# Weights ahead of biases on SyncE, and two of VectorE's products taken apart, in a routed feed-forward kernel

## The reference

```python
t = t + ffn(layernorm(t), Wg, W1, b1, W2, b2)

def ffn(x, Wg, W1, b1, W2, b2):          # 2048 tokens, D=256, E=8 experts, F=1024, TOP_K=2
    S = sigmoid(xt @ Wg)
    G, I = top_k(S, 2)                   # two experts a token, with their gates
    h = gelu(einsum('nd,edf->enf', xt, W1) + b1[:, None, :])
    y = einsum('enf,efd->end', h, W2) + b2[:, None, :]
    combine = zeros((N, E)).at[arange(N)[:, None], I].add(G)
    return einsum('ne,end->nd', combine, y)
```

## Time and profile before

| what | value |
|---|---|
| median of three executions | 346.78 us (346.38 to 348.04) |
| the profiled execution's own time | 349.64 us |
| its span, first to last instruction | 347.8 us |
| PE busy | 301.3 us, 87% of the span |
| DVE busy | 251.8 us, 72% |
| ACT busy | 182.2 us, 52% |
| POOL busy | 155.1 us, 45% |
| bytes moved by DMA | 39.41 MB, 113 GB/s over the span |

### The profile page before, as it was taken

One profiled execution on the slowest core, in us unless ns is written; L12 is line 12 of the kernel. 1 busy time (PEld: TensorE's weight loads), 2 busy tenths in 40 slices (PEclk: granted clock), 3 DMA queues, 4 the chain that ended last, 5 costly groups with the idle time before them and its releaser, 6 DMA issues.

```text
span 347.8 us, 8621 instructions
## 1 busy us (share of the span) xinstructions
PE 301.3 (87%) x3022; PEld 225.6 (65%) x3022; DVE 251.8 (72%) x597; ACT 182.2 (52%) x506; POOL 155.1 (45%) x161
## 2 busy tenths in 40 slices
PE   0989989999920687999999989999999999999970
PEld 0767833557710366788888868888888888877740
DVE  3786789578899869988887798797855655655530
ACT  3344649444653427558576567667544353554410
POOL 7012770337531360454456354644554635444341
PEclk9989999999975699999999999999999999999996
DMA  7400000002286854367888678789454334233310
GB/s 235 145 1 2 1 0 1 2 0 82 69 288 205 160 164 173 97 148 227 190 206 212 158 168 225 214 183 237 90 90 82 66 73 80 49 69 62 57 17 2
DMA packets 36185, 39.41 MB, mean 113 GB/s; under 512 B 8400, under 2 KB 32816, under 8 KB 36144
## 3 DMA queue, kind: packets, MB, share of 16 engines
q1 hardware_dynamic: 29168, 29.56, 29.5%
q0 software_dynamic: 6976, 9.31, 15.9%
HBM read 29.74 MB, written 9.11 MB: 112 GB/s over the span
## 4 chain that ended last, share of the span: by engine, by line
PE 62%; DVE 16%; DMA 11%; issue 4%; ACT 2%; another core or an unknown queue 1%; SPq 1%; POOL 1%; POOLq 0%; ACTq 0%
PE ps L886 14%; PE ps L871 7%; PE ps L875 7%; PE ps L873 7%; PE ps L887 7%; DMA out<-fb,idx 6%; PE ps L731 5%; PE ps L712 3%; DMA wt<-w 2%; DMA xt<-x_tok 2%; PE ps L740 2%; PE ps L744 2%; PE ps L747 2%; PE ps L825 2%; PE ps L779 1%
## 5 line engine op out<-in xcount | busy, mean ns | idle before, releaser
L659 ACT ACTIVATE fb<-ps,b1t 128x128 f32<-128x128 f32 (+7 forms) x312 | 82.1, 381 | 71.6 <-issue 51.4
L871 PE MATMUL ps<-fb,wt 128*128 128x128 f16 (+7 forms) x624 | 114.4, 214 | 5.3 <-DVE fb L1296 5.3
L886 PE MATMUL ps<-wt,fb 128*128 x312 | 117.0, 379 | 0.0
L875 PE MATMUL ps<-fb,wt 128*128 128x128 f16 (+7 forms) x624 | 114.4, 214 | 0.3 <-issue 0.3
L873 PE MATMUL ps<-fb,wt 128*128 128x128 f16 (+7 forms) x624 | 114.3, 214 | 0.0
L523 POOL DMA_INDIRECT out<-fb,idx x39 | 65.3, 1674 | 101.7 <-DMA out<-fb,idx 69.8
L887 PE MATMUL ps<-wt,fb 128*128 x312 | 85.0, 272 | 0.0
L871 PEld LDWEIGHTS ps<-fb,wt 128*128 x624 | 60.9, 98 | 36.0 <-issue 6.2
L873 PEld LDWEIGHTS ps<-fb,wt 128*128 x624 | 60.4, 98 | 3.3
L875 PEld LDWEIGHTS ps<-fb,wt 128*128 x624 | 60.4, 98 | 0.5 <-issue 0.5
L513 POOL DMA_INDIRECT fb<-xn_rows,idx x39 | 43.6, 1117 | 25.0 <-DVE idx L1274 12.8
(11 more groups left out here) (204 smaller groups left out, 388.1 us busy)
## 6 DMA issues: line engine op xcount, KB each, us to landing
wt<-w SPq DMA_DIRECT2D x32, 512.0 KB
b2t<-b SPq DMA_DIRECT2D x39, 128.0 KB
xt<-x_tok SPq DMA_DIRECT2D x4, 512.0 KB, 7.8
out<-xt SPq DMA_DIRECT2D x8, 256.0 KB, 2.1
xn_rows<-wt SPq DMA_DIRECT2D x8, 256.0 KB, 3.3
b1t<-params SPq DMA_DIRECT2D x39, 4.0 KB
fb<-xn_rows,idx POOLq DMA_INDIRECT x39
out<-fb,idx POOLq DMA_INDIRECT x39, 4.0
```

Source lines behind the costliest of these rows:

```text
L659: a = nc.scalar.activation(hid[:, s, f * P:f * P + ROWS[n]], h_ps(s)[:, f * P:f * P + ROWS[n]], ACT.Gelu_apprx_tanh, bias=b1t[:, n % NBIAS ...
L871: pe.matmul(dst, hi, xT[:, s, c * P:c * P + rows], start=(c == 0 and f % 4 == 0), stop=False, skip_group_check=True)
L875: m = pe.matmul(dst, lo, xT[:, s, c * P:c * P + rows], start=False, stop=(c == DC - 1), skip_group_check=True)
L886: pe.matmul(y_ps(s), hhi[:, s, f * P:(f + 1) * P], w, start=(f == 0), stop=False)
```

## The change

Four edits. SP's opening order becomes pieces 0 and 1, the last rows, the biases of tile 0, pieces 2 and 3, the biases of tiles 1 to 3. In SP's loop the pieces of a tile stand ahead of biases, and the biases are those of tile n + 2 in place of n + 3. `quarters_at(1)` is empty, and piece 4 goes to tile 2's turn beside piece 5, on all three engines that read the function. And `gate_pay` makes one product a call, with `rows_T(3)` between the two calls in VectorE's turn 1; in turn 2 it no longer stands.

```diff
-            upto = lambda n: min(QUARTERS_FIRST + 4 * n // 3, NQ)
+            upto = lambda n: min(QUARTERS_FIRST + 4 * n // 3, NQ) if n != 1 else QUARTERS_FIRST
...
-            for h in range(NSTG):
+            for h in range(DC):
                 load(h)
             rows_out(B - 1)
-            for i in range(NBIAS):
+            biases(0)
+            for h in range(DC, NSTG):
+                load(h)
+            for i in range(1, NBIAS):
                 biases(i)
...
             for n in range(1, TILES):
-                if n + NBIAS - 1 < TILES:
-                    biases(n + NBIAS - 1)
                 for h in quarters_at(n):
                     if h + NSTG < NQ:
                         load(h + NSTG)
+                if NBIAS <= n + 2 < TILES:
+                    biases(n + 2)
...
-            def gate_pay():
+            def gate_pay(n):
-                for n in (2, 3):
-                    ins = v.tensor_tensor(out=pay[:, :, n, :], in0=pay[:, :, 0, :],
-                                          in1=over_tiles(flat(place16[:, n]), 2 * NBLK), op=ALU.mult)
-                ins.then_inc(hot_done, 1)
+                return v.tensor_tensor(out=pay[:, :, n, :], in0=pay[:, :, 0, :],
+                                       in1=over_tiles(flat(place16[:, n]), 2 * NBLK), op=ALU.mult)
...
                 if n == 1:
-                    gate_pay()
-                if 2 <= n < TILES - 1:
+                    gate_pay(2)
+                    rows_T(3)
+                    gate_pay(3).then_inc(hot_done, 1)
+                if 3 <= n < TILES - 1:
                     rows_T(n + 1)
```

## The result

| what | before | after |
|---|---|---|
| median of 20 executions each | 348.93 us (346.38 to 350.87) | 345.76 us (345.06 to 348.82) |
| ratio | 1 | **0.9924** [0.9903, 0.9946] |
| the profiled execution's own time | 349.64 us | 345.52 us |
| its span | 347.8 us | 343.7 us |

The change makes the kernel 0.76% faster, about 2.65 us (1.9 to 3.4 by the interval). This ratio and those of the experiments are the ones on record with their intervals; they are not the quotients of the medians beside them (here 345.76 / 348.93 = 0.9909, or 3.17 us).

The account below looks back on a forecast made before the run. PE sets the pace from about 124 us, with VectorE the bound at the start. Forecast: 346.78 - 0.84 (start) - 0.40 (late weights) = 345.5 us; 8-in-10 range 343.9 to 346.9.

Parts of the forecast that it names:

- The start, 0.84 us: Steps 2 to 4, bound by VectorE: the new order lets step 4 start 0.84 us earlier, bounds 0.3 to 1.15.
- The loop: SP's loop: pieces asked for earlier remove the 1.50 us gap ahead of step 14 in the profiled execution.
- I take 0.4 of late weights in the median: Loop's share of the median: 0.4 us of the 1.50, from three runs' spread of 1.66 us; bounds 0 to 1.5.
- rival B: Every execution has a gap like step 14's, at places with two pieces in one tile; median 344.4 us; chance 27%.
- 3.8 a piece: Tile 12's two weight pieces: 7.6 us from issue to ACT's start on the first, read as 3.8 us each.
- 18 of the 19 waits: ACT's other waits for late weight pieces were hidden behind PE's own step and give nothing.
- The opening order, 0: Start of the kernel: pieces 2 and 3 behind rows and biases cost nothing and gain nothing, taken as 0.
- The biases, late but in time: SP's queue: each bias up to 7.6 us later behind two pieces, still in time with 2 us of cover.
- below 4: Sign of being right: ACT's 15.4 us of waiting for weights fall below 4 us.
- C: Rival: the first gelu waited for its bias, so the earlier bias gives 343.8 us; sign, step 2's gap gone; chance 8%.
- D: Rival: adds land late among weights in flight and delay `scaled`; slower, 349.2 us; chance 7%.
- E: Rival: nothing measurable, the 0.84 us is lost again and late weights are rare; 346.4 to 346.8 us; chance 13%.

Follow-up runs that it names:

- e4: Kernel before with only `rows_T(3)` between the two products of `gate_pay`, piece 4 still in turn 1: 347.71 us against 348.22, 0.9991.
- e5: Changed kernel with `gate_pay` in one piece and `rows_T(3)` back in turn 2, turn 1 still empty: 346.11 us against 348.31 of the kernel before, 0.9957.
- e3: Kernel before with only the empty `quarters_at(1)` and the split `gate_pay`, old loop and old opening: 352.46 us against 348.22, 1.0095.
- e7: Changed kernel, but from tile 5 SP's loop also waits for `scaled(n - 1)` before asking for pieces: 368.34 us against 348.31 of the kernel before, 1.0583.
- e11: The kernel before, unchanged, profiled once more: one execution, 349.98 us.
- e8: Changed kernel with 10 filler products in place of 16 ahead of step 0: 347.20 us against 348.31 of the kernel before, 0.9959.
- e2: Kernel before with only SP's loop changed, pieces ahead of biases and biases of tile n + 2: 346.52 us against 348.22, 0.9937.
- e6: Changed kernel with the old opening order: 347.24 us against 348.31 of the kernel before, 0.9953.
- e1: Kernel before with only the opening order changed: 348.25 us against 348.22, 0.9990.
- e9: Changed kernel, from tile 5 issuing biases of tile n + 2, then waiting for `scaled(n - 1)`, then pieces: 346.67 us against 348.69 of the kernel before, 0.9948.
- e10: Changed kernel with the old loop from tile 5, biases of tile n + 3 and then pieces: 347.75 us against 348.69 of the kernel before, 0.9969.

## Why the prediction was right, and where it was not

**The start, 0.84 us: right in mechanism and size.** A is 28.46 to 28.58 (mean 28.50) in the five profiles with a split in turn 1, and 27.54 to 27.86 (mean 27.67) in the seven without: 0.83 us. The reason holds too: 13.08 us between `rows_T(2)` and the end of `rows_T(4)` on both sides, 12.87 of them VectorE's work. Its signs came as told: the gap ahead of step 3 shrank from 1.29 to 0.26 (0.15 forecast); step 4 comes 142.69 - 137.02 = 5.67 us after step 3, 0.17 more than the 5.50 of the next step; and counted from `rows_T(2)` it is 14.20 - 13.34 = 0.86 us earlier. Not seen was what e4 and e5 show: the empty turn 1 earns all of it, and the two products taken apart, which the title names, earn nothing. Nor did the costing say that SP reads the same table, which makes this edit dear without the other (e3).

**The loop: right in mechanism, mis-sized.** The mis-sized term is in the sentence "I take 0.4 of late weights in the median". It read the loss from how far three times lay apart. But a good part of that spread is the clock in the convolution, which comes and goes by about 1.5 us with the old loop and with the new. The losses in B measure the term by itself: with the old loop 1.66, 3.18, 0, 0.53 and 0.53 (mean 1.18; e3 left out), with the new one 0, 0, 0, 0 and 0.62 (mean 0.12; e7 left out). The term is about 1.06 us, between the 0.4 taken and the 1.50 of rival B. Not all of it is late weights: e11's step 16 (0.24 us) with the old loop and e8's 0.62 with the new come behind late adds. That it is the loop's is shown by e2, which has it alone; e3's rows show the path in the large, from a late request to ACT, VectorE and PE.

Two readings behind this term were wrong. "3.8 a piece" halves the 7.6 us between the request for two pieces and ACT's start on the first; but the first alone took them, and a piece asked for by itself was ready in 4.2 (asked for at 182.03, split from 186.27 on). And of the "18 of the 19 waits" that were "hidden behind PE's own step", four lie ahead of the pipeline.

**The sum.** 0.83 + 1.06 = 1.9 us, the low end of the measured 1.9 to 3.4. The rest up to 2.65, 0.75 us, no experiment assigns; five profiles with losses from 0 to 3.18 leave the mean of the loop's term uncertain by more than that. The kernels that leave out only a part that earns nothing, e5 and e6, gained 0.0043 and 0.0047, or 1.5 and 1.6 us, so the 2.65 may be high by chance. The profiled execution's own sum, 347.3 of 349.64, had been nearer (0.9933, inside the interval): adjusting it to a median of three made it worse. But its 1.50 was one draw too, from losses of 0 to 3.18.

**The opening order, 0: right** (e1, e6).

**The biases, late but in time: right.** After shows no wait for a bias. The Trainium skill (DMA: Bandwidth & Descriptors, Queues, rings and completion order) has an engine's ring consumed in order; a later write may finish before an earlier one, but the count that tells of completion waits for all earlier writes of that DMA engine. e7 agrees: in the trace's counts of landings the two pieces asked for at 166.53 count up to 171.49 and 172.84, the bias behind them to 173.20. In e7 a bias behind pieces landed 4.2 us after its own issue by the last count that the trace holds (median, 3.4 to 5.7), one after the last piece 3.6 (3.3 to 4.1). The 7.6 us allowed for two pieces ahead held: from the issue of the pieces at 166.53 to the gelu at 173.22 are 6.7.

**ACT's waits "below 4": wrong as a number.** The 7.4 us that remain are the first four pieces; 15.4 had held 5.6 us of such waits too, and I didn't take them apart.

**Rivals.** B's gap is not in every execution (e1 has none), though its size was nearer than mine, and its places were right: e11 shows a gap at five of the six, so "only one of the six" was an accident of one profile.

C falls: the first gelu begins 11.72 us after the first table in after and 128.61 - 116.80 = 11.81 in before, and from 11.72 to 12.03 in all twelve profiles, with either opening order. The trace's semaphore counts settle it: tile 0's bias had landed by 116.76 in before and 112.49 in after, over 11 us ahead, and the count that ended the wait is PE's own of tile 0's first products, at 128.52 and 126.79, 0.08 us before the gelu. "Remote" only meant that this count came 1.85 us behind the last product as the profile shows it. The gap ahead of step 2 did shrink, from 1.51 to 0.41, which I had named as C's sign: but only because step 0 began later, 8.00 us after the table in place of 6.80, and left a shorter wait behind it; what follows came no sooner for it.

D happened in e8, where it cost 0.62 us, and in e11's step 16 (0.24) with the old loop. Against it, mostly the adds came sooner: POOL waited 31 to 38 us for them in after, e2, e5 and e6 and 59.1 in e8, and 61 to 72 in the six profiles with the old loop. By the same section of the Trainium skill a DMA engine takes turns between queues packet by packet, so weights in flight can delay an add. The trace of before agrees: an add took 5.2 us from issue to landing (median) between 140 and 240 us, among weights, and 3.7 from 245 us on, after the last. So the runs speak not against the rule but against what I made of it: as many bytes are moved, only earlier, and in all but e8 the adds gained clearly. E is out: the interval ends at 0.9946.

## What to carry to other kernels

Let a prefetch wait for what frees its buffer and for nothing else: in a queue of one order, a small transfer that waits for a late consumer holds every request behind it (e2 and e3; whether the earlier request or the place ahead of the bias transfers does it, e9 and e10 leave open). A table that several engines read is an order on each of them, so an edit to it has to be costed on the queue that issues the transfers too. Size a loss that comes and goes from several profiles of the stage it lies in, not from the spread of a few total times, which holds every other accident as well.

## What the runs showed of the hardware

- In four of twelve profiles most of 20 to 24 us ran at 1.2 GHz (granted clock 0.57 to 0.64), in the others at 2.4 GHz (1.00), with PE busy 3.85 us or more of the 4 in all of them. The kernel before shows both; which decides it is open.
- The first gelu begins at a nearly fixed time after the first table (11.72 to 12.03 us), whether step 0 started at 6.7 or at 8.1. What ends ACT's wait is PE's count of tile 0's first products, in all twelve. Where step 0 started early, this count came 1.84 to 1.97 us behind the last product as the profile shows it, and the wait is put down as "remote" (3.52 us in the earlier trace rows); elsewhere 0.11 to 1.05. It isn't the bias; why PE's count comes so late stays open.
- Adds mostly landed sooner when weights were asked for earlier (POOL's waits 69.8 us before, 37.6 after, but 59.1 in e8), with the same 39.41 MB moved.
- An add takes longer among weight transfers: in before 5.2 us from issue to landing (median, longest 8.2) between 140 and 240 us, 3.7 from 245 us on, after the last weights. A bias does too: in e7 4.2 us (median) behind pieces, 3.6 after the last.
